# Second attention scores: two single-precision-rounded matmuls over 128 rows, or one fp32 matmul over 64 rows

## What is computed

```python
q = (x @ Wq).reshape(b, t, H, D).transpose(0, 2, 1, 3)
ckv = x @ Wkva
kv_latent, k_rope = (ckv[:, :, :R], ckv[:, :, R:])
kv = (kv_latent @ Wkvb).reshape(b, t, H, NOPE).transpose(0, 2, 1, 3)
k_rope = jnp.broadcast_to(k_rope[:, None, :, :], (b, H, t, ROPE))
q = jnp.concatenate([q_nope, _rope(q_rope)], axis=-1)
k = jnp.concatenate([kv, _rope(k_rope)], axis=-1)
v = jnp.concatenate([kv, jnp.zeros_like(k_rope)], axis=-1)
att = jnp.einsum('bhqd,bhkd->bhqk', q, k) / jnp.sqrt(jnp.float32(D))
att = jax.nn.softmax(jnp.where(mask, att, -jnp.inf), axis=-1)
y = jnp.einsum('bhqk,bhkd->bhqd', att, v)
```

## Time and profile before

| | us |
|---|---|
| median of 3 runs | 4109.65 |
| lowest and highest | 4104.24, 4113.88 |
| span of the profiled execution | 4099.4 |
| PE busy (its share of the span) | 3512.7 (86%) |
| DVE busy | 3056.1 (75%) |
| ACT busy | 2303.1 (56%) |
| POOL busy | 776.0 (19%) |

### The profile page before, as it was taken

One profiled execution on the slowest core, in us unless ns is written; L12 is line 12 of the kernel. 1 busy time (PEld: TensorE's weight loads), 2 busy tenths in 40 slices (PEclk: granted clock), 3 DMA queues, 4 the chain that ended last, 5 costly groups with the idle time before them and its releaser, 6 DMA issues.

```text
span 4099.4 us, 93010 instructions
## 1 busy us (share of the span) xinstructions
PE 3512.7 (86%) x31392; PEld 2772.0 (68%) x31392; DVE 3056.1 (75%) x6444; ACT 2303.1 (56%) x6346; POOL 776.0 (19%) x919
## 2 busy tenths in 40 slices
PE   3898988989889898898988889888898988989888
PEld 2676766767667676676766767666676766767667
DVE  3878777787777877768787787877778777787776
ACT  2656546565465664646655465654656546565464
POOL 1212222022120221212122121222202212022120
PEclk9999999999899999999999999998999989999899
DMA  3000000000000000000000000000000000000000
GB/s 73 7 2 7 7 7 7 2 7 7 7 7 1 8 6 7 7 7 7 2 7 7 7 7 2 7 7 7 7 2 7 7 7 7 2 7 7 6 1 6
DMA packets 33906, 30.35 MB, mean 7 GB/s; under 512 B 8864, under 2 KB 33312, under 8 KB 33376
## 3 DMA queue, kind: packets, MB, share of 16 engines
q1 hardware_dynamic: 33376, 23.68, 2.0%
HBM read 15.28 MB, written 8.39 MB: 6 GB/s over the span
## 4 chain that ended last, share of the span: by engine, by line
PE 56%; issue 14%; DVE 13%; ACT 10%; POOL 5%; SPq 1%; ACTq 0%; DMA 0%; DVEq 0%; POOLq 0%
PE bank L619 12%; PE scores L717 9%; ACT prob L833 6%; PE bank L630 6%; PE scores L606 6%; PE bank L729 5%; PE scores L607 4%; PE scores L608 3%; POOL qf L499 2%; PE scores L691 2%; PE scores L671 2%; PE scores L602 2%; PE bank L590 2%; DVE negmax L1049 1%; DVE stk L1145 1%
## 5 line engine op out<-in xcount | busy, mean ns | idle before, releaser
L833 ACT ACTIVATE prob<-scores,negmax 128x128 f32<-128x128 f32 (+3 forms) x2048 | 1060.8, 538 | 223.6 <-DVE negmax L1049 180.2
L1049 DVE TENSOR_REDUCE negmax<-scores 128x1 f32<-128x128 f32 (+3 forms) x2048 | 884.5, 483 | 102.0 <-PE scores L608 88.4
L619 PE MATMUL bank<-ident,prob 128*128 128x128 f32 x5120 | 731.2, 280 | 44.5 <-DVE probt L1057 35.1
L1057 DVE COPY probt<-bank 128x512 f32<-128x512 f32 x896 | 596.6, 683 | 180.1 <-PE bank L619 173.1
L619 PEld LDWEIGHTS bank<-ident,prob 128*128 128x128 f32 x5120 | 548.6, 142 | 155.5 <-DVE probt L1057 65.9
L606 PE MATMUL scores<-khh,qt 128*128 128x256 f32 (+2 forms) x1024 | 439.2, 430 | 13.3 <-issue 6.6
L608 PE MATMUL scores<-mask,ident 128*128 128x128 bf16 x2048 | 450.4, 231 | 0.0
L833 ACT ACTIVATION_READ_ACCUMULATOR prob<-scores,negmax 128x1 f32 x2048 | 438.0, 214 | 0.0
L804 ACT ACTIVATE probt<-bank 128x512 f32<-128x512 f32 x384 | 233.0, 607 | 205.3 <-PE bank L619 205.3
L607 PE MATMUL scores<-kll,qt 128*128 128x256 f32 (+2 forms) x1024 | 346.1, 338 | 0.0
L590 PE MATMUL bank<-ident,stk 128*96 128x128 bf16 x2048 | 206.9, 288 | 149.8 <-DVE stk L1147 119.7
(11 more groups left out here) (178 smaller groups left out, 6937.0 us busy)
## 6 DMA issues: line engine op xcount, KB each, us to landing
x_in<-in_x_rows SPq DMA_DIRECT2D x16, 512.0 KB, 3.5
out_rows<-x SPq DMA_DIRECT2D x16, 512.0 KB, 3.5
r_gu<-in_wg SPq DMA_DIRECT2D x2, 512.0 KB, 5.1
r_gu<-in_wu SPq DMA_DIRECT2D x2, 512.0 KB, 5.1
r_d<-in_wd SPq DMA_DIRECT2D x1, 1024.0 KB, 6.5
r_wqt<-in_wq_nope_t SPq DMA_DIRECT2D x1, 512.0 KB, 6.8
r_wqr<-in_wq SPq DMA_DIRECT2D x2, 256.0 KB, 8.6
r_wob<-in_wo SPq DMA_DIRECT2D x1, 512.0 KB, 5.3
```

The lines of the kernel that those rows point to most:

```text
L619: ins = nc.tensor.transpose(bank[4 + n % 2][:, q * P:(q + 1) * P], prob[:, u % 2, q, i * P:(i + 1) * P], ident[:, :])
L833: nc.scalar.activation(prob[:, u % 2, q, 0:n], bank[q][:, 0:n], ACT.Exp, bias=negmax[:, a, u, q:q + 1], accum_out=sums[:, a, u, q:q + 1]). ...
L1049: nc.vector.tensor_reduce(negmax[:, a, u, M * part:M * part + M], scores[:, M * part:M * part + M, 0:n], axis=AX.X, op=ALU.max, negate=Tru ...
L1057: nc.vector.tensor_copy(probt[:, u % 2, i], bank[4 + n % 2][:, :]).then_inc(probt_dve.sem, 1)
```

## The change

Queries and keys are no longer split into a rounded part and a remainder. `stq`, `khh` and `kll` are gone, and with them the ACT copy and the DVE subtraction of each n and POOL's two operations for `kll`. `qf` is transposed as it is, two heads of 64 channels at a time, so that there are 4 transposes per n where there were 8, and one copy per n (ACT for even n, DVE for odd n) where there were two. `qt` holds an even head in rows 0 to 63 and the odd head after it in rows 64 to 127; `kt` holds the key twice, once in each half. The buffers of `qf` come free when PE has transposed them. Each head's scores are one fp32 matmul over 64 rows and exactly n columns, and then the mask as before.

```diff
@@ score
                 else:
-                    m = max(n, 2 * P)
-                    tok = qt[:, h, j * P:(j + 1) * P]
-                    mm(bank[q][:, 0:m], tok, khh[:, 0:m], start=True, stop=False)
-                    mm(bank[q][:, 0:m], tok, kll[:, 0:m], start=False, stop=False)
+                    rows = slice(h % 2 * DK, (h % 2 + 1) * DK)
+                    mm(bank[q][:, 0:n], qt[rows, h // 2, j * P:(j + 1) * P], kt[rows, 0:n], start=True, stop=False)
                 ins = mm(bank[q][:, n - P:n], ident16[:, :], mask16[:, :], start=False, stop=True)
@@ transpose_q
-            pe.wait_ge(qh_ready.sem, qh_ready.at(b, n + 1))
-            pe.wait_ge(ql_ready.sem, ql_ready.at(b, n + 1))
-            for r in range(2):
-                m = 2 * n + r
-                if m >= 3:
-                    copied = qt_dve if (m - 3) % 2 else qt_act
-                    pe.wait_ge(copied.sem, copied.at(b, (m - 3) // 2 + 1))
-                for i in range(4):
-                    ins = nc.tensor.transpose(bank[(4, 5, 7)[m % 3]][:, i * P:(i + 1) * P],
-                                              stq[:, n % 2, 4 * r + i].rearrange("p s d -> p (s d)").bitcast(F32), ident[:, :])
-                ins.then_inc(qt_psum.sem, 1)
+            pe.wait_ge(nope_ready.sem, nope_ready.at(b, n + 1))
+            pe.wait_ge(rope_ready.sem, rope_ready.at(b, n + 1))
+            if n >= 3:
+                copied = qt_dve if (n - 3) % 2 else qt_act
+                pe.wait_ge(copied.sem, copied.at(b, (n - 3) // 2 + 1))
+            for i in range(4):
+                ins = nc.tensor.transpose(bank[(4, 5, 7)[n % 3]][:, i * P:(i + 1) * P],
+                                          qf[:, n % 2, 2 * i:2 * i + 2].rearrange("p h d -> p (h d)"), ident[:, :])
+            ins.then_inc(qt_psum.sem, 1)
@@ ACT, query stretch
-                if 1 <= n <= 2 * NT:
-                    act.wait_ge(rope_ready.sem, rope_ready.at(b, n))
-                    act.wait_ge(nope_ready.sem, nope_ready.at(b, n))
-                    if n >= 3:
-                        act.wait_ge(qt_psum.sem, qt_psum.at(b, 2 * (n - 2)))
-                    copy(stq[:, (n - 1) % 2, :, 0], qf[:, (n - 1) % 2]).then_inc(qh_ready.sem, 1)
@@
-                    copy(khh[0:DK], kf[0:DK])
-                    copy(khh[DK:2 * DK], kf[0:DK]).then_inc(khh_ready.sem, 1)
+                    copy(kt[0:DK], kf[0:DK])
+                    copy(kt[DK:2 * DK], kf[0:DK]).then_inc(kt_ready.sem, 1)
@@ DVE, query stretch
-                if 1 <= n <= 2 * NT:
-                    dve.wait_ge(qh_ready.sem, qh_ready.at(b, n))
-                    s = (n - 1) % 2
-                    tt(stq[:, s, :, 1], qf[:, s], stq[:, s, :, 0].bitcast(F32), ALU.subtract).then_inc(ql_ready.sem, 1)
@@ POOL, query stretch
-                if n == KV_STEP + 6:
-                    pool.wait_ge(khh_ready.sem, khh_ready.at(b, 1))
-                    chain.link(nc.gpsimd.tensor_tensor(kll[0:DK], kf[0:DK], khh[0:DK].bitcast(F32), ALU.subtract))
-                if n == KV_STEP + 7:
-                    nc.gpsimd.tensor_tensor(kll[DK:2 * DK], kf[0:DK], khh[0:DK].bitcast(F32), ALU.subtract).then_inc(kll_ready.sem, 1)
-                    pool.wait_ge(kll_ready.sem, kll_ready.at(b, 1))
```

More of the change, by code:

```diff
@@ L201, in _build @@
     tb = at("tb", [P, 2, 8, R], F32, o + 14336)
-    stq = at("stq", [P, 2, 8, 2, DK], F32R, o + 16384)
     va = new("va", [P, NT, H, HP], F32)
-    khh = new("khh", [P, L], F32R)
-    kll = new("kll", [P, L], F32R)
+    kt = new("kt", [P, L], F32)
     vb = new("vb", [P, NT, R], F32)
@@ L913, in sequence @@
             for n in range(2 * NT + 3):
-                if n >= 3:
-                    m = 2 * (n - 3)
+                if n >= 3 and (n - 3) % 2 == 0:
+                    m = n - 3
                     act.wait_ge(qt_psum.sem, qt_psum.at(b, m + 1))
-                    copy(qt[:, 4 * (m % 4):4 * (m % 4) + 4, (m // 4) * P:(m // 4 + 1) * P],
+                    copy(qt[:, 4 * (m % 2):4 * (m % 2) + 4, (m // 2) * P:(m // 2 + 1) * P],
                          bank[(4, 5, 7)[m % 3]].rearrange("p (h t) -> p h t", h=4)).then_inc(qt_act.sem, 1)
@@ L1165, in sequence @@
             for n in range(2 * NT + 3):
-                if n >= 3:
+                if n >= 3 and (n - 3) % 2:
                     copy_q(b, n - 3)
```

35 lines of the change are left out of this document (15 added, 20 removed).

## The result

| | us |
|---|---|
| before, median of 4 runs beside it | 4111.36 |
| after, median of 4 runs | 4700.88 |
| lowest and highest of after | 4696.23, 4718.22 |
| ratio, with its 95% interval | 1.1455 [1.1414, 1.1496] |
| span of the profiled execution | 4695.9 |

What follows compares the result with a forecast made beforehand. PE was taken to bound attention 2, busy 60.46 of 60.80 us; at the query stretch's end it waits for ACT, DVE and POOL. 4099.4 + 509 - 80 = 4528, plus 10: about 4539 us, 10.4% slower; range 4260 to 4600.

Steps and rivals of the forecast that it cites:

- The format: Attention 2 scores: each fp32 matmul runs as two halves at two cycles per column, 2.13 us a head over four tiles.
- Rival B: Attention 2 scores: a half matmul streams one column per cycle, +0.93 us a head over four tiles, total 4280; chance 0.04.
- The changes of shape: Attention 2, between 64-row scores and 128-row mask: each change costs PE 0.08 to 0.10 us, taken as 0.095.
- Rival A: Attention 2: the 64-row shape changes for free, a head costs 2.77 us over four tiles, total 4281; chance 0.08.
- All terms together: Attention 2 scores: a head over four tiles 3.73 us against 1.79; with 12 us per-unit cost +509, bounds 465 to 550.
- Rival C: Attention 2: two heads run in the array's two halves at once, 0.28 us less a head, total 3958; chance 0.07.
- The query stretch: End of the query stretch: ends 5.0 us earlier per sequence, -80 us over 16 sequences, bounds -37 and -96.
- POOL's addition: Query stretch: POOL's step in the cycle of a `qf` buffer, about 1.1 us within 3.0 us for two steps.
- The step that failed: Attention 2: granted clock taken to remain at 0.95, low only at the start, so no time was added for it.
- rival D: Attention 2: the granted clock falls to 1.2 GHz for the whole stretch, total about 5800 us; chance 0.04.

Runs made afterwards that it cites:

- the pair kernel: Changed kernel with the scores of two heads (rows 0 to 63, then 64 to 127) issued before both their masks: 4120.82 us, ratio 1.0033.
- filled: Ten matmuls without use added in PE's waits at the end of the query stretch: kernel before 4064.46 us, changed kernel 4646.11 us.
- fp32 over 128 rows: Kernel before with each head's scores as one fp32 matmul over all 128 rows, query stretch as before: 4309.74 us, ratio 1.0486.
- zero halves: Changed kernel with two key copies, each zero in the other half, so scores use 128 rows without shape changes: 4209.96 us, ratio 1.0238.
- 128, two per head, in columns: The zero halves kernel with the attention 2 mask written as four matmuls of 128 x 32: 4474.01 us, ratio 1.0926.
- 64, none, one half: Changed kernel without the mask in attention 2 and with every head in rows 0 to 63: 4274.31 us; filled, 4161.39 us.
- 64 in both halves, no masks: Changed kernel without the mask in attention 2, heads in rows 0 to 63 and 64 to 127 in turn: 3999.11 us.
- by fours: Against the pair kernel, all four heads of a unit issued first, then the four masks, and filled: 4290.56 us, ratio 1.0476.
- masks first: Against the pair kernel, the first pair's masks in each unit go ahead of its heads: 4059.92 us, ratio 0.9881; filled, 4017.27 us, ratio 0.9777.

## Why the prediction was wrong in size, point by point

**The format** was right. An fp32 matmul is two rows of the profile, each with two cycles per column (L554's halves lie 214 ns further apart at 512 columns than at 256), on 64 rows as on 128. Rival B, one cycle per column, falls with it: L554's second half to the mask takes 522 ns at 512 columns, where B had 320.

**The changes of shape** were right. The forecast took 0.095 us each from matmuls of 32 rows and 32 columns; from the mask to the next head the trace shows 159 ns (forecast 0.165 with the stream), and the second half to the mask 522 (forecast 0.52). Rival A asked for 0.04 behind the mask and is out. That a change of rows costs what one of columns does was taken without a row of 64, and it held. The Trainium skill (TensorEngine Tiling, Key Properties) says that a change of mode drains TensorE; the 0.25 us for two changes with their loads is its price here. All terms together were a little high, 3.73 us a head against 3.58: -38 us over 256. (The bounds for them were added up short. The single terms' ends give some 440 to 565 us and not 465 to 550, and even with the 550 and the 43 of the query stretch the upper end is 4623 and not 4600. The result lies above that too.)

**Rival C** was right about the array and wrong about this kernel: the halves run at once as soon as no mask stands between them. The prediction named that mask as the point from which C decides, and the pair kernel shows it.

**The query stretch** gave 96 us, 6.0 in each sequence, where 5.0 was taken and 6 was the upper bound. The 5.0 were worked out on the sequence of the earlier trace rows, where the stretch takes 27.1 us from the first projection to the first score, and they came true for it: after the change the mean is 22.1. But the mean before was 28.1. In eight of the 16 sequences the stretch takes 28.8 to 29.4 us; there the clock is at the lower level at its end, and the last eight transposes take 1.94 us where they otherwise take 1.07. That the sequences differ is what the term left out. POOL's addition was mis-sized as well, 1.1 us where it took 0.73 once DVE's subtraction was gone (last section), but that changed little: from the end of the transposes of n = 5 (494.58) to that of n = 7 (497.45) are 2.9 us, where 3.0 were put.

**The step that failed** is the clock of attention 2. The sum took every duration at the level of 0.95 that the earlier trace rows shows, put a fall of the clock at nothing, and gave rival D 4 in 100, and only as a fall over the whole stretch. The argument against D was that the clock stayed at 0.99 at the end of the query stretch with PE idle for a quarter of the time. That argued about waits, and what changed was the work. What it left out can be sized: the scores missed by +151 us, although the terms of a head were 38 too high, which leaves 189 to the clock; 433 us more at the lower level at 0.43 each are 188. The +151 of the scores, the -16 of the query stretch and the +32 of the other stages make +167, and 4528 + 167 = 4695, against the measured span of 4695.9.

**Why it fell**, as far as the runs tell it apart (low in us over 16 sequences):

| rows, changes between heads | unfilled | filled |
|---|---|---|
| 128, none (kernel before) | 86 | 0 |
| 128, none (fp32 over 128 rows; zero halves) | 69; 62 | not run |
| 128, two per head, in columns | 130 | not run |
| 64, none, one half | 290 | 0 |
| 64, two per head (the changed kernel) | 519 | 453 |
| 64 in both halves, no masks | 103 | not run |
| 64 in both halves, by pairs | 100 | not run |
| 64 in both halves, by fours | not run | 92 |
| 64 in both halves, masks first | 75 | 0 |

In these kernels half the rows keep a low clock low, and half the rows with changes of shape between bring a high one down. Over 128 rows with changes the clock, once up, stays up (3 to 10 us low at the start of a sequence and none later), and so it does over 64 rows without changes. The two are not told apart in full: no kernel has 128 rows with a change in rows, and by fours, with both halves used, a high clock falls too, for 7 us. Nor does the changed kernel stay low: in every sequence the clock rises at about the end of the first four units, in the one shown behind 3.8 us of transposes and value matmuls (526.2 to 530.0), and in 14 of 16 it stays high for the last 65 us. What the chip measures to decide it stays open; the table shows only what it did.

## What to carry to other kernels

Before splitting the array in halves, check the order in which the halves are issued: a full-height matmul between them costs two changes of shape (0.25 us with the loads) and takes the overlap away, and moving it behind the pair was worth 580 us of 4701, with what the clock gave back. Price the changes in the program order, and price the clock too: a change that makes each matmul use less of the array can lower the granted clock with PE 100% busy, so look at the granted clock by stretch and not at the busy share alone. Where a dense stretch begins at the lower level behind short waits, a few matmuls without use in them may be worth more than they cost, here 1.1%.

## What the runs showed of the hardware that was not expected

**The lower level with a busy PE.** In the changed kernel PE was busy for 31.52 of 31.60 us at 0.51, and in the filled one the level fell 4 to 9 us after the start, and again later, with PE busy for 92.30 of 92.30 us. I had taken it that only waits bring it down.

**Short waits before a dense stretch.** In the kernel before, waits of 1.42 and 0.83 us at the end of the query stretch go with 86 us at the lower level in attention 2, over all sequences, and with them filled it is 0. PE's order is otherwise the same.

**POOL's addition depends on DVE's work beside it.** All additions of a kernel, by instruction (duration min/median/max), first of the kernel before, then of the changed one:

```profile
L499 POOL TENSOR_TENSOR qf<-ta,tb x128: 728/1066/1117, 190.7 to 3970.0; 128x256 f32<-128x256 f32 x128
```

```profile
L457 POOL TENSOR_TENSOR qf<-ta,tb x128: 721/729/747, 190.1 to 4528.8; 128x256 f32<-128x256 f32 x128
```

In the kernel before, the 16 additions with no DVE subtraction L1180 beside them last 0.73 us on average, the 30 with 0.2 to 0.4 us of it beside them 0.94, and the 82 with 0.4 to 0.6 last 1.09. The subtraction reads two operands from SBUF, while in the changed kernel DVE's copies and products lie beside the additions in part and cost them nothing. The Trainium skill (GPSIMD Engine Reference, Key points) says that GpSimd shares its SBUF interfaces with VectorE and contends with instructions of two SBUF inputs; the trace agrees. The subtraction itself takes 0.68 to 1.31 us.
